# First experts in 10 slots of four 32-place parts, four column strips, and no zero products behind the slots

## What is computed

```python
x = hidden_states.reshape(-1, hidden_shape[-1])        # 1024 tokens of 256, after a layernorm
route = jax.nn.sigmoid(x @ router_w)                   # 8 experts
max_ind = jnp.argmax(route, axis=1)
for e in range(num_experts):
    mask = (max_ind == e)[:, None]
    h = jax.nn.silu(x @ gate_w[e]) * (x @ up_w[e])     # 256 -> 512
    out = out + jnp.where(mask, h @ down_w[e], 0.0)    # 512 -> 256
out = out * max_prob
```

## Time and profile before

| what | us |
|---|---|
| median of 3 runs (740.77 to 741.91) | 741.28 |
| the profiled execution | 739.69 |
| its span in the trace | 738.0 |
| TensorE busy | 715.3 (97%) |
| VectorE busy | 429.1 (58%) |
| ScalarE busy | 347.1 (47%) |
| GpSimd busy | 268.6 (36%) |

### The profile page before, as it was taken

One profiled execution on the slowest core, in us unless ns is written; L12 is line 12 of the kernel. 1 busy time (PEld: TensorE's weight loads), 2 busy tenths in 40 slices (PEclk: granted clock), 3 DMA queues, 4 the chain that ended last, 5 costly groups with the idle time before them and its releaser, 6 DMA issues.

```text
span 738.0 us, 13906 instructions
## 1 busy us (share of the span) xinstructions
PE 715.3 (97%) x4748; PEld 575.9 (78%) x4749; DVE 429.1 (58%) x796; ACT 347.1 (47%) x815; POOL 268.6 (36%) x387
## 2 busy tenths in 40 slices
PE   7999899999899999999999999999999999999997
PEld 6888654444677888899888999888788888888886
DVE  6888574222898755444554445545566665666565
ACT  4888323442677736455454454544532323232333
POOL 3232351111877656312213222121433444344330
PEclk9999999999999999999999999999999999999999
DMA  8980121111200001111010110100034343333421
GB/s 281 419 351 1 30 72 38 47 45 60 78 16 1 24 1 36 28 53 37 21 36 21 57 36 21 64 1 22 22 77 127 99 121 114 113 100 120 126 80 58
DMA packets 23497, 56.36 MB, mean 76 GB/s; under 512 B 3472, under 2 KB 12048, under 8 KB 22432
## 3 DMA queue, kind: packets, MB, share of 16 engines
q1 hardware_dynamic: 22688, 53.72, 22.1%
q0 software_dynamic: 768, 2.10, 0.9%
HBM read 50.49 MB, written 5.31 MB: 76 GB/s over the span
## 4 chain that ended last, share of the span: by engine, by line
PE 84%; ACT 5%; DVE 5%; POOL 3%; DMA 1%; issue 1%; SPq 0%; DVEq 0%; POOLq 0%; ACTq 0%
PE PS L352 17%; PE PS L354 17%; PE PS L353 16%; PE PS L1850 7%; PE PS L1516 6%; PE PS L1537 3%; PE PS L470 3%; PE PS L476 2%; PE PS L516 2%; PE PS L507 2%; PE PS L1856 2%; PE PS L529 2%; POOL Z L854 1%; ACT x_probT L683 1%; PE PS L458 1%
## 5 line engine op out<-in xcount | busy, mean ns | idle before, releaser
L1296 ACT ACTIVATE hhh<-hh 128x512 fp32r<-128x512 f32 x50 | 31.6, 632 | 103.7 <-DVE hh L1318 94.7
L352 PE MATMUL PS<-tTh,wh 128*128 128x512 f32 x200 | 78.3, 392 | 0.8 <-DVE tTl L673 0.5
L353 PE MATMUL PS<-tTl,wh 128*128 128x512 f32 x200 | 77.8, 389 | 0.0
L354 PE MATMUL PS<-tTh,wl 128*128 128x512 f32 x200 | 77.8, 389 | 0.0
L673 DVE TENSOR_TENSOR hhl<-hh,hhh 128x512 fp32r<-128x512 f32 x50 | 52.4, 1047 | 35.4 <-ACT hhh L1296 35.4
L1959 ACT ACTIVATE sm<-sm,nmx 128x128 f32<-128x128 f32 x128 | 49.7, 389 | 37.7 <-DVE nmx L2022 37.7
L1384 POOL CAST wh<-wraw 128x512 fp32r<-128x512 f32 (+1 forms) x50 | 26.1, 523 | 108.6 <-PE PS L354 108.6
L2061 POOL CAST ah<-araw 128x512 fp32r<-128x512 f32 (+1 forms) x32 | 16.2, 506 | 134.4 <-PE PS L354 134.4
L673 DVE TENSOR_TENSOR oTl<-PS,oTh 128x512 fp32r<-128x512 f32 x32 | 22.1, 691 | 71.6 <-ACT oTh L1953 71.6
L1386 POOL TENSOR_TENSOR wl<-wraw,wh 128x512 fp32r<-128x512 f32 (+1 forms) x50 | 58.0, 1161 | 8.4 <-POOL wh L1384 7.9
L352 PE MATMUL PS<-tTh,ah 128*128 128x512 f32 x128 | 53.1, 415 | 0.3 <-POOL al L2063 0.2
(11 more groups left out here) (279 smaller groups left out, 1903.2 us busy)
## 6 DMA issues: line engine op xcount, KB each, us to landing
WE<-moe SPq DMA_DIRECT2D x8, 1536.0 KB, 17.8
wraw<-moe SPq DMA_DIRECT2D x25, 384.0 KB, 3.1
araw<-attn SPq DMA_DIRECT2D x16, 384.0 KB, 3.1
cwb<-cw_d SPq DMA_DIRECT2D x20, 256.0 KB, 3.9
WX<-wx SPq DMA_DIRECT2D x4, 512.0 KB, 6.8
avraw<-attn_v SPq DMA_DIRECT2D x8, 256.0 KB, 3.2
cwb<-cw_d SPq DMA_DIRECT2D x4, 448.0 KB, 3.5
xs_d<-zeros SPq DMA_DIRECT2D x1, 1536.0 KB, 20.5
```

The source lines that it names most:

```text
L352: nc.tensor.matmul(out, wh_, xh_, start=first, stop=False, **kw)
L353: nc.tensor.matmul(out, wh_, xl_, start=False, stop=False, **kw)
L354: return nc.tensor.matmul(out, wl_, xh_, start=False, stop=last, **kw)
L1296: nc.scalar.activation(hhh[half][:, :], hh[half][:, :], ACT.Copy).then_inc(s.hi_done, 1)
```

## The change

A place part has now 32 places. 1024 / 32 + 8 = 40 parts, TILES, fill 10 slots of four (PARTS). Every product of a slot runs in four column strips of 32 columns with four sets of weights; the first is read from WE, three are copied. The copies are whole matrices of 128x1024 (GU). Gate copies for slot j+1: VectorE two, GpSimd one, released by the gate product of slot j. Up copies for slot j+1: ScalarE three, released by the up product of slot j. Down copies for slot j: GpSimd three, released by the down product of slot j-1; the copies of slot 0 and the down copies of slot 9 are shared among the engines in other ways. The copies need more room: w2 grows to six matrices, others use WX[0] (free after the first cross attention) and FX; y_s moves to FX. The two calls of `fill` named above go.

```diff
-HP = P // 2
-HALVES = T // HP + E0
-SLOTS = HALVES // 2
+PARTS = 4
+HP = P // PARTS
+TILES = T // HP + E0
+SLOTS = TILES // PARTS
+GU = C * I0
@@ SBUF
-        w2 = sb("w2", [P, EW], where=e)
+        w2 = sb("w2", [P, 6 * GU], where=e)
+        part_weights = [[WX[0][:, q, :, :].rearrange("p c n -> p (c n)") for q in range(2)] + [w2[:, 0:GU]],
+                        [w2[:, k * GU:(k + 1) * GU] for k in (1, 4, 5)],
+                        [w2[:, k * GU:(k + 1) * GU] for k in (2, 3)] + [FX[:, 0:I0 // P, :].rearrange("p k n -> p (k n)")]]
-        y_s = [sb(f"y_s{i}", [P, D], where=e) for i in range(2)]
+        y_s = [FX[:, I0 // P + i, :] for i in range(2)]
@@ query_squares
-                if b == 1:
-                    fill(4, 4 + turn_no[L]["Q2", b] % 4)
@@ TensorE, up
+                if mat == 0:
+                    pe.wait_ge(s.gate_copied, 2 * j + 2)
+                    pe.wait_ge(s.gate3_copied, j + 1)
+                else:
+                    pe.wait_ge(s.up_copied, 3 * j + 3)
                 for c in range(C):
-                    a0 = (mat * C + c) * I0
-                    out, x = PS[:, 2 * mat + par, :], xsT[par][:, c, :]
-                    nc.tensor.matmul(out[0:HP, :], x[:, 0:HP], expert_part(e, a0, I0), start=(c == 0), stop=(c == C - 1))
-                    pe.wait_ge((s.gate_copied, s.up_copied)[mat], 2 * j + c + 1)
-                    m = nc.tensor.matmul(out[HP:P, :], x[:, HP:P], w2[:, a0:a0 + I0], start=(c == 0), stop=(c == C - 1))
+                    for q in range(PARTS):
+                        w = expert_part(e, (mat * C + c) * I0, I0) if q == 0 else part_weights[mat][q - 1][:, c * I0:(c + 1) * I0]
+                        m = nc.tensor.matmul(PS[q * HP:(q + 1) * HP, 2 * mat + par, :], xsT[par][:, c, q * HP:(q + 1) * HP], w, start=(c == 0), stop=(c == C - 1))
@@ TensorE, down
                     if k == 0:
-                        pe.wait_ge(s.down_copied, j + 1)
-                    m = nc.tensor.matmul(out[HP:P, :], src[:, k, HP:P], w2[:, a0:a0 + D], start=(k == 0), stop=(k == I0 // P - 1))
+                        pe.wait_ge(s.down_copied, 3 * j + 3)
+                    for q in range(PARTS):
+                        w = expert_part(e, 2 * GU + k * D, D) if q == 0 else down_weights(j)[q - 1][:, k * D:(k + 1) * D]
+                        m = nc.tensor.matmul(PS[q * HP:(q + 1) * HP, 6 + par, 0:D], src[:, k, q * HP:(q + 1) * HP], w, start=(k == 0), stop=(k == I0 // P - 1))
@@ TensorE, behind the slots
-                if i == MOST:
-                    pe.wait_ge(s.kt_free, 3)
-                    fill(14, 2)
@@ ScalarE, tile and start
-                e = None if is_last(j) else half_expert(act, j + 1, 1)
+                es = [] if is_last(j) else [part_expert(act, j + 1, q) for q in range(1, PARTS)]
...
+                    act.wait_ge(s.u_done, j + 1)
+                    for q, e in enumerate(es):
+                        part_copy(nc.scalar, e, 1, q + 1, s.up_copied)
...
-            gate_copies(half_expert(act, 0, 1))
+            es = [part_expert(act, 0, q) for q in (3, 2)]
+            part_copy(nc.scalar, es[0], 0, 3, s.gate3_copied)
             columns(0, 0)
+            part_copy(nc.scalar, es[0], 1, 3, s.up_copied)
+            part_copy(nc.scalar, es[1], 1, 2, s.up_copied)
@@ VectorE, tile
-                e = None if is_last(j) else half_expert(dve, j + 1, 1)
+                if not is_last(j):
+                    es = [part_expert(dve, j + 1, q) for q in (1, 2)]
+                    dve.wait_ge(s.g_done, j + 1)
+                    for q, e in enumerate(es):
+                        part_copy(v, e, 0, q + 1, s.gate_copied)
+                else:
+                    dve.wait_ge(s.g_done, j + 1)
+                    dve.wait_ge(s.down_copied, 3 * j)
+                    part_copy(v, part_expert(dve, j, 1), 2, 1, s.down_copied, j)
                 dve.wait_ge(s.u_done, j + 1)
                 dve.wait_ge(s.silu_done, j + 1)
                 v.tensor_tensor(hs[:, :], gs[par][:, :], PS[:, 2 + par, :], ALU.mult).then_inc(s.h_ready, 1)
-                if not is_last(j):
-                    up_copies(e)
                 if is_first(j):
+                    part_copy(v, part_expert(dve, 0, 1), 2, 1, s.down_copied)
                     keys_values(4, MOST)
@@ VectorE, start
+            es = [part_expert(dve, 0, q) for q in (1, 2)]
             keys_values(0, 1, False)
             dve.wait_ge(s.w_in, 16 * E0)
-            up_copies(half_expert(dve, 0, 1))
+            for q, e in enumerate(es):
+                part_copy(v, e, 0, q + 1, s.gate_copied)
+            part_copy(v, es[0], 1, 1, s.up_copied)
@@ GpSimd, tile and start
                 if is_first(j):
                     keys_power(0, MOST, 1)
                 if not is_last(j):
-                    e = half_expert(pool, j + 1, 1)
-                    pool_wait(pool, s.d_done, j + 1)
-                    down_copies(e)
+                    e = part_expert(pool, j + 1, 3)
+                    pool_wait(pool, s.g_done, j + 1)
+                    part_copy(nc.gpsimd, e, 0, 3, s.gate3_copied)
+                if is_last(j):
+                    es = [part_expert(pool, j, q) for q in (2, 3)]
+                    pool.wait_ge(s.g_done, j + 1)
+                    for q, e in enumerate(es):
+                        part_copy(nc.gpsimd, e, 2, q + 2, s.down_copied, j)
+                elif not is_first(j):
+                    es = [part_expert(pool, j, q) for q in range(1, PARTS)]
+                    pool_wait(pool, s.d_done, j)
+                    for q, e in enumerate(es):
+                        part_copy(nc.gpsimd, e, 2, q + 1, s.down_copied)
...
-            down_copies(half_expert(pool, 0, 1))
+            part_copy(nc.gpsimd, part_expert(pool, 0, 2), 2, 2, s.down_copied)
+            pool.wait_ge(s.scattered, 16 * B)
+            part_copy(nc.gpsimd, part_expert(pool, 0, 3), 2, 3, s.down_copied)
```

More of the change, by code:

```diff
@@ L969, in routing_constants @@
                 nc.gpsimd.memset(upto[:, e, e:], 0.0)
-            for j in range(HALVES):
+            for j in range(TILES):
                 nc.gpsimd.memset(tile_ids[:, j:j + 1], float(j))
@@ L1446, in slots, with part_expert, down_weights, part_copy @@
                 single(j)
-        def half_expert(eng, j, h):
-            return eng.value_load(ex[0:1, bass.ds(2 * j + h, 1)], min_val=0, max_val=E0 - 1)
+        def part_expert(eng, j, q):
+            return eng.value_load(ex[0:1, bass.ds(PARTS * j + q, 1)], min_val=0, max_val=E0 - 1)
+        def down_weights(j):
+            return part_weights[0 if is_last(j) else 2]
+        def part_copy(eng, e, mat, q, done, j=0):
+            dst, src = (down_weights(j) if mat == 2 else part_weights[mat])[q - 1], expert_part(e, mat * GU, GU)
+            if eng is nc.scalar:
+                m = eng.activation(dst, src, ACT.Copy)
+            else:
+                m = eng.tensor_copy(dst, src)
+            m.then_inc(done, 1)
         def expert_part(e, a0, n):
@@ L1611, in tile @@
                 if is_first(j):
-                    gate_copies(e)
                     hidden_columns(0)
                     columns(1, 1)
-                    return
-                if not is_second(j):
-                    hidden_columns(j - 1)
-                if not is_last(j):
-                    columns(j + 1, 1 - par)
-                    gate_copies(e)
-            def gate_copies(e):
-                for c in range(C):
-                    nc.scalar.activation(w2[:, c * I0:(c + 1) * I0], expert_part(e, c * I0, I0), ACT.Copy).then_inc(s.gate_copied, 1)
+                else:
+                    if not is_second(j):
+                        hidden_columns(j - 1)
+                    if not is_last(j):
+                        columns(j + 1, 1 - par)
+                if not is_last(j):
+                    act.wait_ge(s.u_done, j + 1)
+                    for q, e in enumerate(es):
+                        part_copy(nc.scalar, e, 1, q + 1, s.up_copied)
             act.wait_ge(s.experts_done, 1)
             act.wait_ge(s.w_in, 16 * E0)
-            gate_copies(half_expert(act, 0, 1))
+            es = [part_expert(act, 0, q) for q in (3, 2)]
+            part_copy(nc.scalar, es[0], 0, 3, s.gate3_copied)
             columns(0, 0)
+            part_copy(nc.scalar, es[0], 1, 3, s.up_copied)
+            part_copy(nc.scalar, es[1], 1, 2, s.up_copied)
             slots(act, tile)
@@ L1699, in ffn_dve @@
             ch.link(v.scalar_tensor_tensor(out=ends[:, :], in0=starts[:, :], scalar=1.0 / HP, in1=tiles_of[:, :], op0=ALU.mult, op1=ALU.add))
-            ch.link(v.tensor_tensor(below[:, :, :], ends[:, :].unsqueeze(1).broadcast_to([P, HALVES, E0]),
-                                    tile_ids[:, :].unsqueeze(2).broadcast_to([P, HALVES, E0]), ALU.is_le))
+            ch.link(v.tensor_tensor(below[:, :, :], ends[:, :].unsqueeze(1).broadcast_to([P, TILES, E0]),
```

(14 more changed lines are left out.)

19 lines of the change are left out of this document (7 added, 12 removed).

## The result

| | before | after |
|---|---|---|
| median, us | 741.6 (4 runs, 740.77 to 743.08) | 734.09 (4 runs, 733.03 to 735.54) |
| the profiled execution, its span | 739.69, 738.0 | 733.03, 731.3 |
| TensorE busy | 715.3 | 702.7 |
| GpSimd busy | 268.6 | 302.0 |

The ratio is 0.9898, with an interval of 0.9873 to 0.9923: 7.5 us less, where 8.2 were forecast, and 734.1 us for a forecast of 733.1.

The account below looks back on a forecast made before the run. TensorE, busy for 97% of a 738.0 us span, was taken as the bound. Slots -12.24, start +4.1, end -0.6 and copy brushes +0.5 gave -8.2 us, so a median of 733.1 us, range 729.5 to 739.

Parts of the forecast that it names:

- Two slots and four strips: Routed stage: four column strips share a step, a slot still costs 6.12 us, so two slots fewer save 12.24 us.
- Copies inside the slots: Nine weight copies per slot mostly hide under TensorE; VectorE and GpSimd take turns, 0.5 us in all for brushes.
- The middle case: Within a slot, one VectorE gate copy slips in before GpSimd's third down copy; down weights arrive just in time.
- G + 4.27: G is the start of a slot's gate product; down weights forecast ready 4.27 us later, plus a semaphore, due at 4.39.
- the rival of the turns: Both VectorE copies precede the third down copy; TensorE waits 0.6 us in each of eight slots: 737.5 us, chance 0.17.
- The start: First two slots, where nothing has a lead: longer VectorE and GpSimd queues cost +4.1 us, bounds 1.5 and 6.
- the routing's 0.28: Routing ahead of the slots, on twice the starts and 40 ids: +0.28 us from two operations before the places.
- The end: Last slot: down product no longer waits 1.31 us, hidden rows some 0.8 later; net -0.6 us, from -1.3 to +0.5.
- The zero products: Behind the slots and at the second queries' squares: removal saves nothing, leaves TensorE idle 3.62 us, no clock fall.
- The rival: Clock: the idle 3.62 us behind the slots halve TensorE's rate; +2.5 to 6, taken 4: 737 us, chance 0.15.
- The bounds of start and end: First two slots 1.5 to 6 us, last slot -1.3 to +0.5; together they gave 729.5 to 735.5 us.
- the fourth rival: The change does nothing: the first slots take 10 us more as every start wait lengthens; 741 us, chance 0.03.

Follow-up runs that it names:

- the shared start without zero products: Changed kernel with hidden rows ahead of VectorE's copies (first, last slot), two start copies on ScalarE, GpSimd's gate copy before the keys' power; no zero products: 731.26 us.
- the shared start: Changed kernel with both zero-product calls back, two start copies on ScalarE, hidden rows ahead of VectorE's copies in first and last slot: 729.9 us, again 730.04.
- the reordered start: Changed kernel with two orders swapped in slot 0: VectorE's hidden rows before its gate copies, GpSimd's gate copy before the keys' power: 734.58 us.
- the last three runs: On one chip: changed kernel unaltered again, 734.93 us; its start rearranged with ScalarE taking two copies, without zero products 731.26 us, with them 730.04 us.

## Why the prediction was right, and where it was not

- **Two slots and four strips: right.** A slot stays at 6.10 us, so two are 12.2. The row of four strips with 128 moving columns carried over to 512. The Trainium skill, TensorE: Matmul & The Clock Gate, section on measured speedup against the span model, has four row strips at 3.07 times the speed of one, from which the prediction's estimate was 1.56 us more on each slot. In this stream a step of four took 0.42 to 0.43 us, and the measurement decides.
- **Copies inside the slots: the mechanism right, the size too high.** The middle case came: one VectorE copy gets in ahead of the third down copy. I had a waiting engine lose a whole copy of the other (down weights at G + 4.27); it lost 0.46 us (1.50 for 1.04), and they were there at G + 3.94. VectorE's copy was estimated at 0.70, ScalarE's at 1.0; they took 0.68 and 1.05. The 0.5 us for these meetings was nothing, and the rival of the turns (0.17) stayed out: the down product starts 0.43 us after its last copy is there.
- **A term that was not in the sum.** One slot of the middle takes 6.43 us (134.23 to 140.66 between turnings), where the slots before and behind take 6.10. The down product's last step starts at 138.28, and the gate product, due 0.22 us after it, only at 138.81. With twelve slots there are two such places; before the change none, with as many slots in loops. It is at the back edge of TensorE's loop over slot pairs, by its place; why it costs now and not then is only argued.
- **The start: right in each link, 0.6 us short in the sum** (4.7 with the routing's 0.28, for 4.1). Forecast and measured: hidden rows +2.2 and +2.5, gate product of slot 1 +0.9 and +1.1, up to slot 2 +0.7 and +0.8. The gate product of slot 1 was forecast near 114.45 and came at 115.36, that of slot 2 near 119.3 and at 119.90; 0.4 of either is what the first line of the table has over its forecast, by the clock ahead of the slots. The routing's +0.28 is exact where the clock holds: from TensorE's turning of x_cx, ahead of the routing, to the permuted tokens it is 13.72 us before, 14.00 in the shared start without zero products.
- **The end: right in sign, inside its bounds.** -0.6 was forecast, -1.0 measured. The down product doesn't wait; the hidden rows do, 0.40 us.
- **The zero products: wrong.** The step that failed is "I take no fall, since products come before and after the gap". I had seen that the gap is twice any other, had the row of the slow first zero products beside it, and still took the calls for nothing because no one waits for them. The rival was named with 4 us; it costs 1.2 to 2.3 in a profile and 1.2 to 1.4 in medians, since the half rate lies on few and short products: 0.62 and 0.52 of clock over 4 us, of which TensorE worked 3.3. The forecast held in spite of it because the size was small: of the 1.5 us between the spans of forecast and profile 1.2 are this, 0.6 the start and 0.4 the clock ahead of the slots, and the slots and the end gave 0.6 back. That the total came within 1.0 us is thus luck in part: a mechanism that I had ruled out turned out cheap here, and two terms erred the other way.
- **Two slips in the working.** The bounds of start and end give 729.8 to 736.1, not 729.5 to 735.5. In the fourth rival 10 us for the first slots, put in place of the 4.1, make 739 and not 741: the whole gain is gone only at 12.3. Neither touches the forecast.

## What to carry to other kernels

Work that nobody waits for can still carry the time: before taking out a filler, look at how long the engine stands idle without it, and at what runs in the microseconds behind. When a stage is repeated, price its first and last pass by themselves; in the middle nine copies a slot were free, while at the start two copies taken over by an engine with nothing to do, with the order changed, gave 2.4 us back. Look at the clock in windows of a few us and not in the 40 slices of the page, also before a loss behind a wait is put down to the wait.

## What the runs showed that I had not expected

**A fall of the clock ahead of the slots, in some executions.** From 86 to 89 us on, after a wait of 0.56 us in work that the change doesn't touch, the clock was at one half for three to seven microseconds: granted 0.83 over 85 to 95 us in the first profile of the changed kernel, 0.66 in the second, and 1.00 in three other kernels of four parts and in both of two parts.

```profile
85.00:95.00 10.00, 9.43 (x31) 0.66 0.21 54
```

(the second profile of the changed kernel). The stretch from the turning of x_cx to the permuted tokens took 14.00 us with a full clock, 14.66 with 0.83 and 16.0 to 16.2 with 0.66: up to 2.2 us by chance of the execution. The +0.64 of the table's first line is this 0.66 and the routing's 0.28, less 0.30 by which the work ahead of x_cx came earlier. The runs of before lie between 0.993 and 1.00 of mean clock, so there is room for such falls in them too; in neither profile of two parts did one show, in eight of eleven with four parts it did. Whether the change makes them likelier stays open.

**A wait without a releaser in slot 0.** In eight of the eleven profiles of four parts ScalarE's first activation starts 2.3 us (once 3.7) later than the gate product allows, and the profile names "remote" for it:

```profile
105.74 0.60 ACT L1624 ACTIVATE gs<-PS 128x512 f32<-128x512 f32 x1 [2.39 <-remote]
```

In the second profile of the same kernel it is not there ([0.38 <-PE PS L1536] in its place). In the changed kernel it costs nothing, as VectorE is busy until 108.4 us anyway: both profiles take 76.61 us for the slots. Where the hidden rows come first on VectorE it lies open: of three profiles of the shared start, the one with this wait takes 75.33 us, those without 74.25 and 74.00. It also stands in front of the reordered start above and may explain its loss in part. It isn't tied to the four parts: in the kernel before without the zero products VectorE's hidden rows wait 3.89 us, and the profile says "remote" there too. The three profiles of four parts without it are those of the last three runs, all on one chip, so it may hang on the chip; no run separates this. It comes while GpSimd scatters the tokens; what it is was not found out.
